# Load and projections of a four-layer kernel in one block: x in quarters, keys of both batches in one job, values last

## What is computed

```python
q = x @ Wq + bq                       # 256 -> 256: 32 heads of 8
k = x @ Wk + bk                       # 256 -> 64:   8 heads of 8
v = x @ Wv + bv                       # 256 -> 64
q, k = _rope(q), _rope(k)             # y*cos + (halves swapped)*(+-sin)
att = softmax(causal(q k^T / sqrt(8)))
x = _layernorm(x + (att @ v) @ Wo + bo)
x = _layernorm(x + ffn0(x))
x = _layernorm(x + delta_rule_attention(x))
x = _layernorm(x + ffn1(x))
```

## Time and profile before

| | before |
|---|---|
| median of 3 runs | 2073.97 us (2073.57 to 2085.83) |
| the profiled execution | 2075.61 us |
| its span, first to last instruction | 2073.8 us |
| TensorE busy | 1917.8 us (92%) |
| VectorE busy | 1641.0 us (79%) |
| ScalarE busy | 1300.4 us (63%) |
| GpSimd busy | 739.1 us (36%) |
| mean granted TensorE clock | 0.957 of full |

### The profile page before, as it was taken

The page is one execution under the profiler, slowest core; times in us unless marked ns, Lnnn a source line. Parts: engine busy times, 40 slices in busy tenths (PEclk is TensorE's granted clock), DMA queues, the critical chain, the costliest instruction groups (busy, mean ns, idle before and its releaser), DMA issues. The chain is left out here.

```text
span 2073.8 us, 64658 instructions
## 1 busy us (share of the span) xinstructions
PE 1917.8 (92%) x27132; PEld 1440.7 (69%) x27132; DVE 1641.0 (79%) x3085; ACT 1300.4 (63%) x2822; POOL 739.1 (36%) x1005
## 2 busy tenths in 40 slices
PE   6589999998995799999999999999999999999777
PEld 4133333334784688888888888888888888888666
DVE  3699999982654678888888888988888888888456
ACT  1158888885432457667666666666766766766543
POOL 2333444444222223423433433432432432432223
PEclk9779999999996899999999999999999999999879
DMA  4301212111001011011011111111111111110011
GB/s 144 89 21 36 54 32 60 41 30 30 1 1 40 32 34 46 32 36 46 32 36 38 41 36 36 43 36 36 43 35 36 43 35 36 33 35 15 1 44 41
DMA packets 74175, 79.57 MB, mean 38 GB/s; under 512 B 13280, under 2 KB 60768, under 8 KB 73888
## 3 DMA queue, kind: packets, MB, share of 16 engines
q1 hardware_dynamic: 73888, 75.44, 12.4%
HBM read 66.11 MB, written 8.91 MB: 36 GB/s over the span
## 5 line engine op out<-in xcount | busy, mean ns | idle before, releaser
L1758 DVE SCALAR_TENSOR_TENSOR d_acc<-ps,d_par,d_acc 128x1023 f32<-128x1023 f32 (+2 forms) x288 | 363.6, 1262 | 15.7 <-ACT d_acc L1639 13.8
L1455 PE MATMUL ps<-x1p,d_wh 128*128 128x512 f32 x1024 | 357.9, 431 | 14.1 <-DVE d_acc L1758 9.6
L549 ACT ACTIVATE a_prob<-ps 128x512 f32<-128x512 f32 (+2 forms) x640 | 311.3, 560 | 90.7 <-PE ps L515 86.7
L571 DVE TENSOR_REDUCE a_mx<-ps 128x2 f32<-128x1024 f32 (+2 forms) x320 | 336.6, 1110 | 34.2 <-PE ps L499 21.6
L1639 ACT ACTIVATE d_acc<-ps,d_par 128x512 f32<-128x512 f32 x192 | 148.9, 776 | 141.4 <-PE ps L1455 137.2
L1389 POOL TENSOR_TENSOR d_og_l<-d_o_g,d_og_h 128x512 fp32r<-128x512 f32 x64 | 82.5, 1290 | 354.2 <-ACT d_og_h L1735 354.2
L1455 PE MATMUL ps<-x1p,d_wl 128*128 128x512 f32 x512 | 204.4, 399 | 0.0
L1455 PEld LDWEIGHTS ps<-x1p,d_wh 128*128 128x128 f32 x1024 | 172.7, 193 | 38.0 <-DVE d_acc L1758 10.5
L494 PE MATMUL ps<-k,q 48*128 48x512 bf16 (+3 forms) x768 | 142.5, 347 | 35.9 <-DMA k<-scratch_k 20.7
L515 PE MATMUL ps<-q,k 51*128 51x512 bf16 (+2 forms) x640 | 161.1, 365 | 6.1 <-ACT a_prob L549 3.7
L529 PE MATMUL ps<-a_prob,a_v 128*32 128x512 f32 (+3 forms) x1536 | 166.0, 505 | 0.2
(11 more groups left out here) (242 smaller groups left out, 4791.4 us busy)
## 6 DMA issues: line engine op xcount, KB each, us to landing
d_abc<-scratch_alpha SPq DMA_DIRECT2D x32, 512.0 KB
d_gb<-scratch_g SPq DMA_DIRECT2D x32, 512.0 KB, 3.9
d_wr<-in_dw SPq DMA_DIRECT2D x16, 512.0 KB, 4.9
scratch_q<-p_parts SPq DMA_DIRECT2D x24, 128.0 KB, 2.3
q<-scratch_q SPq DMA_DIRECT2D x32, 96.0 KB
scratch_y<-a_oT SPq DMA_DIRECT2D x64, 36.0 KB
x_tok<-in_x SPq DMA_DIRECT2D x2, 1024.0 KB
q<-scratch_q SPq DMA_DIRECT2D x32, 64.0 KB
```

What stands on the lines that cost most here:

```text
L549: inc(nc.scalar.activation(prob[:, y % PB, g:g + heads, off:], ps[:, PLACE["st", n, x], 0:heads * w].rearrange("p (h c) -> p h c", c=w), A ...
L571: inc(nc.vector.tensor_reduce(out, ps[:, bank:bank + 2, 0:heads * w].rearrange("p r (h c) -> p r h c", c=w), AX.X, ALU.max, negate=True), ...
L1455: last = nc.tensor.matmul(ps[:, bank, :], wp[g][:, k, i, :], x(part), start=(k == 0 and j == 0), stop=(k == KE - 1 and j == 2))
L1758: inc(nc.vector.scalar_tensor_tensor(acc[i][:, d:T], taps[:, 0:T - d], par[p][:, 4 * i + j:4 * i + j + 1], acc[i][:, d:T], ALU.mult, ALU.a ...
```

## The change

The block of constants is gone. `load_and_project` issues ident first, then x in quarters with a semaphore each, then what the keys need, what q needs, what the values need, and the other constants. Transposes use four PSUM banks. The keys of both batches go in one job: batch 0 to output partitions 0 to 63 and batch 1 to 64 to 127. So there are two key jobs (both ahead) and eight q jobs, by batch: ten in all. The values' matmuls come last, with two wide bias adds. The ring of rot, rest and parts has three places, ScalarE's mid part of a job comes ahead of its high part of the next, and VectorE's low part moves one job later. SyncE issues the first unit's six k loads after the stores of job 5 and its six q loads after those of job 7; for that the loads are a function, `fetch_unit`, with q first and then k.

```diff
+def fetch_unit(sp, cst, dram, n, arrived, what):
+    b, kv, p = n // HKV, n % HKV, n % len(cst["q"])
+    for part, (first, count) in enumerate(Q_RUNS):
+        for r in range(2):
...
+            if what == "q":
...
+                sp.dma_start(cst["q"][p][s, :, :], src).then_inc(arrived, 16)
+            else:
...
@@ load_and_project
-        rot = sb("p_rot", [P, 2, HALF])
-        rest = sb("p_rest", [P, 2, HALF])
-        parts = sb("p_parts", [P, 2, 3, HALF], BF16)
+        RING = 3
+        rot = sb("p_rot", [P, RING, HALF])
+        rest = sb("p_rest", [P, RING, HALF])
+        parts = sb("p_parts", [P, RING, 3, HALF], BF16)
...
-        kinds = [("q", 0), ("q", 1), ("k", 0)]
-        jobs = [(kind, c, n) for kind, c in kinds for n in range(NB)]
+        jobs = [("k", 0, 0), ("k", 0, 1)] + [("q", c, 2 * b + n) for b in range(B) for c in range(2) for n in range(2)]
...
             for m, (kind, c, n) in enumerate(jobs):
...
+                if m == 5:
+                    sp.wait_ge(v_clear, 2 + len(cst["k"]))
+                    for o in (0, 1):
+                        sp.wait_ge(stored[o % RING], 48 * (o // RING + 1))
+                    fetch_unit(sp, cst, dram, 0, cst["first_in"], "k")
+                if m == 7:
+                    for o in (2, 3):
+                        sp.wait_ge(stored[o % RING], 48 * (o // RING + 1))
+                    fetch_unit(sp, cst, dram, 0, cst["first_in"], "q")
...
-                if g == 0:
-                    pe.wait_ge(x_in, 32)
-                if g >= 2:
-                    pe.wait_ge(xT_done_act if g % 2 == 0 else xT_done_dve, g // 2)
+                if k == 0:
+                    pe.wait_ge(x_in[t4], 16)
+                if g >= 4:
+                    pe.wait_ge(xT_done_act if g % 2 == 0 else xT_done_dve, g // 2 - 1)
...
+                if m == 0:
+                    pe.wait_ge(k_in, 16 * (3 + B))
...
+                            for b in range(B):
+                                t = b * T + n * HALF
+                                last = nc.tensor.matmul(ps[b * KR:(b + 1) * KR, bank, :], wk[:, k, s, :], xT[:, k, t:t + HALF],
+                                                        start=(k == 0), stop=(k == KE - 1))
...
                 if m >= 1:
                     split(m - 1)
-                    split_low(m - 1)
+                if m >= 2:
+                    split_low(m - 2)
+            dve.wait_ge(cst["in"], cst["in_n"])
+            nc.vector.tensor_copy(cst["step"][:], cst["step_in"][:]).then_inc(made, 1)
+            nc.vector.tensor_scalar(cst["hidden"][:], cst["hidden_in"][:], BIG, None, ALU.mult).then_inc(made, 1)
+            split_low(len(jobs) - 2)
             split(len(jobs) - 1)
+            dve.wait_ge(v_clear, 2)
+            dve.wait_ge(v_in, 32)
+            values(0)
             split_low(len(jobs) - 1)
+            values(1)
@@ attention, sync
-        for n in range(NB):
+        for n in range(1, NB):
             load(n)
```

More of the change, by code:

```diff
@@ L162, in _ @@
                 last.then_inc(v_ready, 1)
[L163 to L171, removed]
         @block.gpsimd
         def _(pool):
+            nc.gpsimd.memset(cst["pow_half"][:], -0.5).then_inc(made, 1)
             nc.gpsimd.memset(v_aug[:], 0.0).then_inc(v_clear, 1)
@@ L180, in _ @@
             pool.wait_ge(v_clear, 2 + len(cst["k"]))
-            for m, (kind, c, n) in enumerate(jobs):
-                r = rows[kind]
+            for m in range(len(jobs)):
                 pool.wait_ge(rotated, 2 * m + 2)
-                if m >= 2:
-                    pool.wait_ge(high_left, m - 1)
-                nc.gpsimd.tensor_tensor(rot[0:r, m % 2], t1[0:r, m % 2], t2[0:r, m % 2], ALU.add).then_inc(summed, 1)
+                if m >= RING:
+                    pool.wait_ge(high_left, m - RING + 1)
+                nc.gpsimd.tensor_tensor(rot[:, m % RING], t1[:, m % 2], t2[:, m % 2], ALU.add).then_inc(summed, 1)
         @block.scalar
@@ L192, in _, with middle @@
                 act.wait_ge(transposed, g + 1)
-                nc.scalar.activation(xT[:, k, t4 * HALF:(t4 + 1) * HALF], ps[:, g % 2, :], ACT.Copy).then_inc(xT_done_act, 1)
-            for m, (kind, c, n) in enumerate(jobs):
-                r = rows[kind]
-                act.wait_ge(summed, m + 1)
[L197 to L201, removed]
+                nc.scalar.activation(xT[:, k, t4 * HALF:(t4 + 1) * HALF], ps[:, g % 4, :], ACT.Copy).then_inc(xT_done_act, 1)
+            def middle(m):
+                act.wait_ge(high_left, m + 1)
+                nc.scalar.activation(parts[:, m % RING, 1], rest[:, m % RING], ACT.Copy).then_inc(mid, 1)
+            for m in range(len(jobs)):
+                if m >= 1:
+                    middle(m - 1)
+                act.wait_ge(summed, m + 1)
+                if m >= RING:
+                    act.wait_ge(stored[m % RING], 48 * (m // RING))
+                nc.scalar.activation(parts[:, m % RING, 0], rot[:, m % RING], ACT.Copy).then_inc(high, 1)
+            middle(len(jobs) - 1)
         @block.vector
@@ L395, in load @@
                 return
-            b, kv, p = n // HKV, n % HKV, n % NB
             W("st", n - NB, NST)
[L398 to L404, removed]
+            for what in "qk":
+                fetch_unit(sp, cst, dram, n, qk_in[n % NB], what)
         def rows(n):
@@ L2119, in build @@
                          {"wq": a["wq2"], "wk": a["wk2"], "wv": a["wv"], "bq": a["bq2"], "bk": a["bk2"], "bv": a["bv"],
-                          "cos": a["c_cos"], "sin": a["c_sin"]}, (w0, ow, hw))
+                          "cos": a["c_cos"], "sin": a["c_sin"], **{n: a["c_" + n] for n in ("ident", "step_in", "hidden_in", "above", "upto", "below")}},
+                         (w0, ow, hw))
         with phase(nc) as joint:
```

123 lines of the change are left out of this document (65 added, 58 removed).

## The result

The changed kernel takes 2060.65 us in the median of its runs (2058.22 to 2066.26), the kernel before 2075.41 beside it (2073.57 to 2085.83): a ratio of 0.9913, 95% interval 0.9889 to 0.9936. It is faster by 0.9%, 15 us, where 27 were forecast, and the time lies outside the stated range (2040 to 2057). The profiled execution took 2066.26 us with a span of 2064.5, so it is one of the slower ones of its kernel (its span is 9.3 us shorter than that of before).

The account below looks back on a forecast made before the run. The first attention matmul, held by the work before it, was taken to set everything behind. Moving it from 91.9 to 64.8 us saves 27.1: 2073.97 - 27.1 = 2047 us; likeliest 2044 to 2051 (0.60), range 2040 to 2057.

Parts of the forecast that it names:

- First key matmul at 13.4: Start: x asked for at 1.26 us, the keys' weights and tables behind it; first key matmul at 13.4 us.
- Two key jobs in 7.2 us: Projections: both batches' 64-column matmuls run side by side, 3.6 us a job; two jobs 7.2 us where four took 14.4.
- that rival: Key jobs: the 64-column pairs don't overlap, everything behind comes 6.5 us later, 2053.5 us; chance 0.13.
- Pace 3.60: q jobs: 3.60 us each, as VectorE's low part still ends behind GpSimd's add; TensorE's 3.43 is the other end.
- Stores: SyncE's stores in the projections: 0.60 us to issue, 0.62 with gap, 1.9 for a job's three; landing 2.3 us.
- a first attention matmul at 71 or later: Sign that the prediction is wrong; the forecast start of attention was 64.8 us, before it was 91.88.
- SyncE's tail of 15.6 us and 3.0 to the barrier's end: From job 5's stores at 46.2 us SyncE is never free for 15.6; 3.0 more to the first attention matmul, 64.8.
- No wait for k at the start of attention, the rest moved as one: Start of attention: TensorE waits only for the barrier; everything behind comes 27 us earlier, clock back 36 us after the start.
- The clock rival: Attention: TensorE's clock stays at 1.2 GHz over 13 us longer, up to half a microsecond each; 2053 to 2074, chance 0.12.

Follow-up runs that it names:

- cut stores: The changed kernel with each key store cut in two, one for each batch: 2051.26 us, ratio 0.9861 to the kernel before.
- loads spread: Changed kernel with key stores cut, GpSimd's add waiting for VectorE's low part, first unit's loads two behind each of jobs 3 to 8: 2054.68 us, ratio 0.9869.

## Why the prediction was wrong, step by step

- **First key matmul at 13.4: right** (13.37), and on the transfer that it named, the last table behind x.
- **Two key jobs in 7.2 us: right** (7.09). The 64-column halves run side by side; that rival is out.
- **Pace 3.60: right.** L279 stands at 24.18, 27.79 and 31.39. The reason holds too: L261 lasts 1.76 us behind the add (about 1.3 was expected), and 0.68 once the add waits. In the Trainium skill, "SBUF — State Buffer", section "Who interferes with whom", the two block each other for whole instructions. The trace agrees: L261 ends 0.55 us behind the add (27.87 against 27.32), as forecast, and lasts 1.76 us against 0.68. So VectorE and GpSimd meet not only at semaphores.
- **Stores: here it failed.** "A store takes 0.60 us to issue, 0.62 with its gap, 1.9 for a job's three", and the landing of 2.3, were measured on stores led by 64 rows or 16 heads, and used for a store of another shape, led by 2. At 48 GB/s the three key stores of a job (0.39 MB) take 8 us on two engines. The ring of three carried it to ScalarE (8.11 and 6.13 us), from there to VectorE and TensorE. The clock fell meanwhile and stretched one q job to 6.44 us, but that job was done at 48.3 and VectorE took it up only at 52.18, so it cost nothing. Job 5's low part ended at 55.9 instead of 46.2: 9.7 of the 9.9 us that the start was late by. In the terms of the sum nothing stood for the key stores' transfer and the waits that it makes, where 9.7 us belonged; with the stores cut, the start came at 65.57, 0.8 us behind the forecast, and the time at a ratio of 0.9861, where 0.987 was forecast. The prediction had itself named a first attention matmul at 71 or later as a sign of being wrong; it came at 74.71.
- **SyncE's tail of 15.6 us and 3.0 to the barrier's end: right.** From 55.9 to 74.7 are 18.8 us, 18.6 forecast. (Two slips in the working changed nothing: by its own terms SyncE reaches job 9 at 60.6, not 60.2, and x with only its own bytes gives a first key matmul at 12.6, not 12.8.)
- **No wait for k at the start of attention, the rest moved as one: right up to 443 us.** The first matmul waits for the barrier only, and the lead of 17.2 us is 16.6 at the last maxima. The clock is back 38 us after the start, not 36.
- **The clock rival: right in kind, at another place.** It was priced at up to half a microsecond for each at 1.2 GHz and looked for in the first units. It came at attention's end, 20.5 us at 1.2 GHz where before had 3.4, for 6.4 us more, or 0.37 us for each. This size is also what the runs of one kernel differ by, so it belonged into the range from the start.

The median of after is 14.8 us better: 27.1 minus 9.9 at the start, and minus 2.4 more. Falls of the clock as in the profiled execution could make up these 2.4 us, but for the timed runs that isn't shown.

## What to carry to other kernels

When a store or load is merged over one more dimension, look at which dimension then leads on each side: here the bytes stayed, and the engines that carried them went from sixteen to two. A cost read off a row holds for the shape in that row. And where runs of a kernel differ by 7 us, a 1.5 us gain at the start needs the trace, not the clock on the wall, to be seen.

## What the hardware showed that was not expected

- Stores of 128 KB led by 2 run at 48 GB/s and a DMA share of 0.14, those of 64 KB at 42 and 0.13. The same bytes in stores led by 64 land in 2.1 us each.
- The six stores of 128 KB also held SyncE longer, 1.06 us in the median and up to 3.05 to issue, against 0.60 before; those of 64 KB led by 2 did not (0.49 us).
- A leading 2 whose step joins with the next dimension costs nothing: landing 2.1 us.
- The same work at the end of attention takes 38.0 to 45.0 us, by how long the clock is low in it. TensorE had been idle for 1.5 us in executions of either kind (cut stores 38.0, loads spread 45.0).
